# A GRU, attention, RK4 and FFN kernel: FFN pieces in new slots on all engines, a seed between two transposes, one piece ahead of the cubic term

## The reference, cut to what matters

```python
def derivative(q, p, drive, coupling, bias):
    dq = q - q ** 3 / 3.0 - p + drive + jnp.tanh(q) @ coupling.T + bias
    dp = EPSILON * (q + ALPHA - BETA * p)
# four derivatives a step (RK4), then q and p are clipped; 64 steps; q is kept
...
qx, sx, sc = reorder_quantize(q_trace, up_reorder_index)      # fp8 by row
g = qlinear(qx, sx, sc, w_gate, ...)                          # 512 -> 1408
u = qlinear(qx, sx, sc, w_up, ...)
t = jax.nn.silu(g) * u
qt, st, sct = reorder_quantize(t, down_reorder_index)
y = qlinear(qt, st, sct, w_down, down_reorder_index)          # 1408 -> 512
out = x1 + y
```

## Time and profile before

| | us |
|---|---|
| runs (3), median | 1643.82 |
| lowest, highest | 1642.74, 1644.45 |
| the profiled execution's own time | 1640.76 |
| its span | 1638.8 |

### The profile page before, as it was taken

One profiled execution on the slowest core, in us unless ns is written; L12 is line 12 of the kernel. 1 busy time (PEld: TensorE's weight loads), 2 busy tenths in 40 slices (PEclk: granted clock), 3 DMA queues, 4 the chain that ended last, 5 costly groups with the idle time before them and its releaser, 6 DMA issues.

```text
span 1638.8 us, 46339 instructions
## 1 busy us (share of the span) xinstructions
PE 1489.4 (91%) x16583; PEld 927.8 (57%) x16624; DVE 1119.8 (68%) x3565; ACT 588.7 (36%) x1903; POOL 381.5 (23%) x545
## 2 busy tenths in 40 slices
PE   5999999996799999999999997678899999999984
PEld 1333333334575767667675844556666666666662
DVE  1667667765774747575664732578888888888886
ACT  1444444441102020201102021455555555555552
POOL 0221221210000000000000000245655555556550
PEclk8999999997899999999999998999999999999996
DMA  7111112116101000100000024001111111111111
GB/s 304 44 45 50 51 46 65 51 47 167 9 1 26 0 26 0 26 0 26 6 19 13 13 64 163 21 25 29 40 40 40 33 35 32 35 32 43 37 38 33
DMA packets 91035, 72.79 MB, mean 44 GB/s; under 512 B 32480, under 2 KB 82912, under 8 KB 89824
## 3 DMA queue, kind: packets, MB, share of 16 engines
q1 hardware_dynamic: 71184, 59.35, 12.4%
q10 hardware_dynamic: 18032, 6.88, 1.7%
q0 software_dynamic: 1760, 5.77, 1.2%
HBM read 55.03 MB, written 16.94 MB: 44 GB/s over the span
## 4 chain that ended last, share of the span: by engine, by line
PE 73%; DVE 13%; ACT 5%; issue 5%; DMA 1%; POOL 1%; DVEq 0%; SPq 0%; POOLq 0%; ACTq 0%
PE ps L655 13%; PE ps L645 13%; PE ps L750 11%; PE ps L583 11%; PE ps L595 10%; PE ps L689 3%; PE ps L713 3%; ACT mem L961 3%; DVE mem L1313 2%; DVE mem L1271 2%; PE ps L740 2%; ACT ps L953 2%; PE ps L764 1%; PE ps L666 1%; DVE ps L1281 1%
## 5 line engine op out<-in xcount | busy, mean ns | idle before, releaser
L750 PE MATMUL ps<-mem 128*32 128x128 f32 x8192 | 278.8, 276 | 68.5 <-ACT mem L961 65.8
L750 PEld LDWEIGHTS ps<-mem 128*32 128x32 f32 x8192 | 211.4, 110 | 143.0 <-ACT mem L961 97.2
L645 PE MATMUL ps<-mem 128*128 128x512 f32 x512 | 224.6, 592 | 0.0
L655 PE MATMUL ps<-mem 128*128 128x256 f32 x1024 | 222.3, 379 | 0.0
L655 PEld LDWEIGHTS ps<-mem 128*128 128x128 f32 x1024 | 194.0, 190 | 26.0
L509 POOL TENSOR_TENSOR mem<-mem 128x128 f32<-128x128 f32 x64 | 30.8, 481 | 732.8 <-ACT mem L956 732.8
L583 PE MATMUL ps<-mem 128*32 128x384 f32 x2048 | 181.6, 497 | 10.2 <-DMA mem<-in_W_ih 6.3
L595 PE MATMUL ps<-mem 128*32 128x384 f32 x2048 | 177.6, 488 | 2.4 <-DVE mem L1098 2.4
L928 ACT ACTIVATE mem<-mem 128x512 f32<-128x512 f32 x32 | 19.7, 630 | 391.0 <-DVE mem L1211 391.0
L645 PEld LDWEIGHTS ps<-mem 128*128 128x128 f32 x512 | 95.6, 190 | 109.7 <-issue 109.3
L961 ACT ACTIVATE mem<-mem 128x64 f32<-128x64 f32 x512 | 102.9, 248 | 116.5 <-DVE mem L1271 116.4
(11 more groups left out here) (139 smaller groups left out, 2097.0 us busy)
## 6 DMA issues: line engine op xcount, KB each, us to landing
mem<-x_scr SPq DMA_DIRECT2D x128, 64.0 KB, 1.8
mem<-in_xT SPq DMA_DIRECT2D x64, 64.0 KB, 1.9
mem<-in_Wq SPq DMA_DIRECT2D x1, 4096.0 KB, 12.4
mem<-in_Wo SPq DMA_DIRECT2D x1, 4096.0 KB, 20.7
mem<-in_x SPq DMA_DIRECT2D x16, 256.0 KB, 2.8
x_scr<-mem SPq DMA_DIRECT2D x32, 128.0 KB, 2.3
q_scr<-mem SPq DMA_DIRECT2D x64, 64.0 KB, 1.6
mem<-q_scr SPq DMA_DIRECT2D x64, 64.0 KB, 1.9
```

Of the source, the lines that this page charges most:

```text
L645: mm = pe.matmul(ps[:, 6 + pr, :], aoT[:, h, pr * P:pr * P + P], wo[:, h, :], start=(h == 0), stop=(h == HEADS - 1))
L655: mm = pe.matmul(ps[:, h % Q_BANKS, 0:BLK], wq[:, c, h * DH:(h + 1) * DH], xnb[:, c, :], start=(c == 0), stop=(c == NC - 1))
L750: mm = pe.matmul(ps[32 * j:32 * j + 32, st % 2, 0:P], thT[:, c, :], ct[:, c, j * P:(j + 1) * P], start=False, stop=(c == NC - 1), skip_gro ...
```

## The change

The products become pieces by a table of (product, first, last matmul) for each slot. PE: slot 11 also takes two matmuls of the second product, slot 12 its other two and two of the third, slot 13 the rest; slot 0 takes one matmul of the sixth product and slot 1 three. The down product is cut 2, 5, 3, 1 instead of 3, 3, 3, 2. The parts of t change sizes (640, then 768 columns). On DVE `gate_part` 1 goes from slot 13 to 14, `t_added` 0 from 11 to 10, `t_grid` 1 from 10 to 11, `t_added` 1 from 15 to 13, `ysc` from 10 to 15. On GpSimd and ACT the matching pieces move (second `gate_scaled` and `silu_part` 14 to 15, roundings 12 to 11 and 15 to 14, the output's addition 11 to 15). SP puts the output's store and x1's loads behind the tile's loads. In the RK4, DVE does a first stage's `fill()` ahead of the cubic term, and the seed of a step's first stage between the two transposes.

```diff
-GU_SLOTS = (11, 12, 13, 15, 0, 1, 3, 4)
-DOWN_SLOTS = (5, 7, 8, 9)
-T_PARTS = ((0, 6 * P), (6 * P, INNER))
+GU_SLOTS = {11: ((0, 0, NC), (1, 0, 2)), 12: ((1, 2, NC), (2, 0, 2)), 13: ((2, 2, NC),), 15: ((3, 0, NC),),
+            0: ((4, 0, NC), (5, 0, 1)), 1: ((5, 1, NC),), 3: ((6, 0, NC),), 4: ((7, 0, NC),)}
+DOWN_SLOTS = {5: (0, 2), 7: (2, 7), 8: (7, 10), 9: (10, IC)}
+T_PARTS = ((0, 5 * P), (5 * P, INNER))
...
-                    if s == 2 and out_tile is not None:
-                        tile_store(out_tile)
-                    if s == 2 and x1_tile is not None:
-                        tile_x1(x1_tile)
                 if g is not None:
                     tile_loads(g)
+                if out_tile is not None:
+                    tile_store(out_tile)
+                if x1_tile is not None:
+                    tile_x1(x1_tile)
...
-                    if k in (13, 14):
-                        gate_scaled(i, k - 13)
+                    if k in (13, 15):
+                        gate_scaled(i, k // 15)
...
-                    if k in (12, 15) and rk:
-                        t_rounded(i, k // 15)
+                    if k in (11, 14) and rk:
+                        t_rounded(i, k // 14)
...
-                if i is not None and k == 11 and rk:
+                if i is not None and k == 15 and rk:
                     pool.wait_ge(f_ysc, i + 1)
...
-                    if k == 8:
+                    if k == 7:
                         pe.wait_ge(f_tTcp, 2 * i + 2)
                     if k in DOWN_SLOTS:
-                        down(i, DOWN_SLOTS.index(k))
+                        down(*DOWN_SLOTS[k])
...
-                    if k in (13, 14):
-                        silu_part(i, k - 13)
+                    if k in (13, 15):
+                        silu_part(i, k // 15)
...
+            def turned_half(src, half):
+
+                dve.transpose(qsT[:, 2 * half:2 * half + 2, :].rearrange("p c b -> p (c b)"), src[:, half * 64:half * 64 + 64]).then_inc(rk_qT, 1)
+
             def state_turned(src):
-
-                for half in range(2):
-                    dve.transpose(qsT[:, 2 * half:2 * half + 2, :].rearrange("p c b -> p (c b)"), src[:, half * 64:half * 64 + 64]).then_inc(rk_qT, 1)
+                turned_half(src, 0)
+                turned_half(src, 1)
...
+                if st == 0:
+                    fill()
                 dve.wait_ge(rk_sq, n + 1)
                 stt(out=ebuf, in0=ps[:, 5, 0:P], scalar=KEPT[st], in1=qs, op0=ALU.subtract, op1=ALU.mult).then_inc(rk_e, 1)
                 if st < 3:
                     seed(t, s, st + 1)
-                fill()
-                if st == 0 and not (last and s == 3):
+                if st:
+                    fill()
+                elif not end:
                     drive_sum(t + 1, (s + 1) % 4, g + 1 + (s == 3))
...
-                if not (end and st == 3):
+                if st < 3:
                     state_turned(dst)
-                if st == 3:
+                else:
                     if not end:
+                        turned_half(dst, 0)
                         seed(t + 1, (s + 1) % 4, 0)
-
+                        turned_half(dst, 1)
                     wait_if(dve, q_wr[s], PRIMED + 16 * g)
                     dve.tensor_scalar(qn[s], dst, CLAMP, -CLAMP, ALU.min, ALU.max).then_inc(rk_qs, 1)
...
-                    if k in (12, 13):
-                        if k == 12:
-                            v.need(v.n)
-                        gate_part(i, k - 12)
+                    if k == 12:
+                        v.need(v.n)
+                        gate_part(i, 0)
                     if k == 14:
+                        gate_part(i, 1)
                         gated_part(i, 0)
...
                     if k == 10:
+                        t_added(v, 0)
+                    if k == 11:
                         t_grid(v, 1)
-                    if k == 11:
-                        t_added(v, 0)
-                    if k == (15 if rk else 11):
+                    if k == (13 if rk else 11):
                         t_added(v, 1)
...
-                if i is not None and k == 10:
+                if i is not None and k == (15 if rk else 10):
                     v.need(v.n)
                     dve.wait_ge(f_y, i + 1)
```

More of the change, by code:

```diff
@@ L754, in stage, with product @@
                     mix_into(t, s, st + 1)
-            def product(i, kind, m):
-                gate, order = kind == "g", GU_ORDER.index((kind, m))
-                wait_if(pe, *{0: (f_gated, GU_T * i - 1), 1: (f_gated, GU_T * i), 2: (f_gsc, GU_T * i + 1), 3: (f_gsc, GU_T * i + 2),
-                              4: (f_gated, GU_T * i + 1), 5: (f_gsc, GU_T * i + 3), 6: (f_gated, GU_T * i + 2),
-                              7: (f_gsc, GU_T * i + 4)}[order])
-                for c in range(NC):
+            def product(i, order, lo, hi):
+                kind, m = GU_ORDER[order]
+                gate = kind == "g"
+                if lo == 0:
+                    wait_if(pe, *{0: (f_gated, GU_T * i - 1), 1: (f_gated, GU_T * i), 2: (f_gsc, GU_T * i + 1), 3: (f_gsc, GU_T * i + 2),
+                                  4: (f_gated, GU_T * i + 1), 5: (f_gsc, GU_T * i + 3), 6: (f_gated, GU_T * i + 2),
+                                  7: (f_gsc, GU_T * i + 4)}[order])
+                for c in range(lo, hi):
                     mm = pe.matmul(ps[:, 2 + order % 2, 0:GU_N], qxT[:, c, :], (wgT if gate else wuT)[:, c, m * GU_N:(m + 1) * GU_N],
                                    start=(c == 0), stop=(c == NC - 1))
-                mm.then_inc(f_g if gate else f_u, 1)
+                if hi == NC:
+                    mm.then_inc(f_g if gate else f_u, 1)
             def t_turned(i, half):
@@ L788, in slot @@
                         pe.wait_ge(f_qTcp, i + 1)
-                    if k in GU_SLOTS[:4]:
-                        product(i, *GU_ORDER[GU_SLOTS.index(k)])
+                    if k >= 11:
+                        products(i, k)
                 i = tile(1)
                 if i is not None:
-                    if k in GU_SLOTS[4:]:
-                        product(i, *GU_ORDER[GU_SLOTS.index(k)])
+                    if k < 11:
+                        products(i, k)
                     if k == 15:
@@ L803, in slot, with products, down @@
                         pe.wait_ge(f_tTcp, 2 * i + 1)
-                    if k == 8:
+                    if k == 7:
                         pe.wait_ge(f_tTcp, 2 * i + 2)
                     if k in DOWN_SLOTS:
-                        down(i, DOWN_SLOTS.index(k))
-            def down(i, part):
-                for c in range(3 * part, min(3 * part + 3, IC)):
+                        down(*DOWN_SLOTS[k])
+            def products(i, k):
+                for order, lo, hi in GU_SLOTS.get(k, ()):
+                    product(i, order, lo, hi)
+            def down(lo, hi):
+                for c in range(lo, hi):
                     mm = pe.matmul(ps[:, 7, :], t8T[:, c, :], wdT[:, c, :], start=(c == 0), stop=(c == IC - 1))
-                if part == 3:
+                if hi == IC:
                     mm.then_inc(f_y, 1)
```

## The result

| | before | after |
|---|---|---|
| median of 4 runs each, us | 1643.28 | 1624.84 |
| lowest, highest | 1640.08, 1644.45 | 1623.2, 1630.71 |
| ratio to before, 95% interval | | 0.9908, 0.9887 to 0.9928 |
| the profiled execution's own time | 1640.76 | 1630.71 |
| its span | 1638.8 | 1628.8 |

What follows compares the result with a forecast made beforehand. The prediction took a loop of dependences through PE, DVE and ACT as the bound. 13.3 us from 12 loop passes plus 3.9 outside make 17.2, off the median of 1643.82: 1626.6 us, range 1618 to 1637.

Steps and rivals of the forecast that it cites:

- The loop's term: The device loop's 12 passes: each falls from 36.27 to 35.16, 1.11 less, 13.3 us in all.
- The forecast case: Whole kernel: mask collides with GpSimd's addition but goes before its next operation, seed shortens the step's end; 1626.6 us, chance 0.52.
- The step's end: Last stage of a step: with the seed between the transposes, coupling to coupling takes 2.15 instead of 2.26.
- The second rival: At the steps' ends the seed gains nothing: 5.3 us missing, 1631.9 us, or 1636.7 with a late half; chance 0.18.
- The first stage's piece: First stages of steps: FFN piece ahead of the cubic term, so DVE is no longer late; 2.16 instead of 2.39.
- Stage 0: First stage of a pass: 2.16 plus 0.15 for a fifth product matmul, 2.31.
- The products: Second stages (1, 5, 9, 13): one or two matmuls fewer, so each takes the floor of 2.13; stage 1 had 2.25.
- Stage 8: First stage with the bit mask as its piece: mask overlaps GpSimd's addition, takes about 1.0, and the stage takes 2.72.
- The first rival: In stage 8 the mask does not collide with GpSimd's addition: stage 2.23, 5.9 us less, 1620.7 us; chance 0.15.
- The third rival: In stage 8 GpSimd's next operation goes ahead of the waiting mask: 1.43 more a pass, 1645.7 us; chance 0.07.
- GpSimd's two places: GpSimd's delayed first multiply and its longer rounding before the step's sum: 0.06 in stage 14, 0.07 in stage 15.
- Outside the loop: Four passes outside the loop: group 0 nothing, group 1 0.25, groups 2 and 15 1.8 each; together 3.9 us.

Runs made afterwards that it cites:

- seed_back: The changed kernel with its two transposes together again and the seed behind them; 1626.25 us, pass 35.36 against 35.19.
- before_piece: The kernel before with only a first stage's piece put ahead of the cubic term; 1635.27 us, beside 1641.82 for the kernel before.
- later_and_spread: Changed kernel, both masks in stage 9, grids in 10, first addition in 11, one matmul moved from stage 0 to 15, one from 7 to 6; 1616.29 us.
- mask_back: The changed kernel with stage 8's bit mask alone put back behind the cubic term and the seed; 1640.59 us, beside 1640.79 for the kernel before.

## Why the prediction was right, point by point

Forecast 1626.6 us, measured 1624.84 and, timed again, 1624.43. The loop's term was 13.3 and came out as 13.24 in one execution and 13.13 in the other. The forecast case holds: the mask does collide, GpSimd does not keep its turn, the seed does shorten the step's end.

- **The step's end**: 2.15 forecast; 2.15, 2.20, 2.16 and 2.15 measured in stages 3, 7, 11 and 15. The 0.93 from the new state to the coupling is exact. The second rival (the seed gives nothing) falls, for the step's end. But two things about the clip were off. The forecast had it "0.12 before the now earlier coupling", and it starts 0.06 before: from the first transpose to the clip, start to start, it takes 0.54 (1265.54 to 1266.08) with the seed between the transposes, and took 0.48 (1301.79 to 1302.27) with the pair in one. And the rival's price, 4 x 0.11 x 12 = 5.3 us, left out that a clip nearer to the coupling makes the next first stage longer, a loss that the seed brings and that would go with it. seed_back shows it: the four steps' ends lose 0.37 by undoing the seed, the four first stages get 0.23 back, 0.14 of it in stage 0, and with 0.02 in stage 14 about 0.17 a pass is left, 2.0 us in the loop.
- **The first stage's piece**: 2.16 forecast for stages 4 and 12, 2.15 measured, and 2.12 to 2.16 in before_piece. Right, and the later clip does not show here because the mixes start 0.34 behind the seed L1303 (as in the rows above, 1267.08 to 1267.42) and not the 0.41 that was taken as an upper bound.
- **Stage 0** was the mis-sized term: 2.31 forecast, 2.45 measured in every steady pass. Its mixes were put at +1.15 or so and start at +1.28. The working had L1303 at +0.77, and it is at +0.94 (1266.14 to 1267.08): 0.06 from the clip, and 0.12 more between clip and piece than in other stages. In stage 12 of the pass the piece starts 0.17 behind the clip, in stage 0 it starts 0.30 behind:

```profile
1257.47 0.25 DVE L1341 TENSOR_SCALAR mem<-ps 128x128 f32<-128x128 f32 x1
...
1257.64 0.56 DVE L1451 SCALAR_TENSOR_TENSOR mem<-ps,mem 128x352 f32<-128x352 f32 x1
...
1547.54 0.25 DVE L1341 TENSOR_SCALAR mem<-ps 128x128 f32<-128x128 f32 x1
...
1547.72 0.56 DVE L1451 SCALAR_TENSOR_TENSOR mem<-ps,mem 128x352 f32<-128x352 f32 x1
```

  The second pair is stage 0 of group 15, which is written out behind the loop: 0.18. The first pass, entered from above, has 0.18 too (1125.47, 1125.65), and its stage 0 takes 2.27. What sets the steady passes apart is DVE's branch back to the loop's start: the last register instruction of the loop (its line is `Fori`'s, L104) is at 1266.2 in the steady pass, behind the clip's start, and at 1125.2 in the first, ahead of it. Before, the branch lay in the 0.35 that DVE idled for ACT's square; the piece ahead of the cubic term used that cover up. A loop written out was not tried, so the branch is argued from where the 0.12 appears and where not. Against the forecast it is 0.14 x 12 = 1.7 us.
- **The products**: 2.13 forecast for stages 1, 5, 9, 13, and 2.13 in each. Stage 7: 2.18 forecast, 2.20 measured. The price of the fifth matmul in stage 0, 0.15, is shown by later_and_spread.
- **Stage 8**: 2.72 forecast, 2.67 measured, the mask 1.00 long for "about 1.0", ending 0.34 behind L539 for the 0.35 taken. The first rival (no collision) falls. The reading to the letter of the Trainium skill's rule (SBUF — State Buffer, section Who interferes with whom) was 0.1 more: the second of a pair waits until the first has ended and then runs whole, which would be 0.48 behind L539 and not 0.34. That one blocks the other for a whole instruction, and that the order of issue decides, the traces bear out: in mask_back the mask takes 1.60 for 0.48 where the subtraction goes first, and the subtraction 1.63 for 1.27 where the mask does. The 0.05 by which the stage came out shorter is the bound of 0.41 again: the mixes start at +1.60 (1283.62 to 1285.22) and not at +1.69.
- **The third rival** (GpSimd keeps its turn) falls by the rows of after, in which the waiting mask goes first in every pass. Its price was never met: 1.43 a pass was for a mask that waits from the clip on through both of GpSimd's operations. The nearest case that was run, a mask that asks just behind the subtraction (mask_back), costs 0.93.
- **GpSimd's two places**: 0.06 in stage 14 was right (2.19), and by the first of the two queues that the forecast named. In stage 13 GpSimd's L510 takes 1.02 under DVE's wide addition (in before it took 0.46 there), so its multiply L525 ends only at 1262.48; DVE's product with it, L1459, starts 0.11 behind that, and the new state L1327 at +1.28 (1261.81 to 1263.09) for +1.22:

```profile
1260.03 1.02 POOL L510 TENSOR_TENSOR mem<-mem 128x128 f32<-128x128 f32 x1 [1.60 <-ACT mem L964]
...
1261.54 0.94 POOL L525 TENSOR_TENSOR mem<-mem 128x352 f32<-128x352 f32 x1
...
1261.81 1.08 PE L751 MATMUL ps<-mem 128*32 128x128 f32 x32
...
1262.59 0.58 DVE L1459 SCALAR_TENSOR_TENSOR mem<-ps,mem 128x352 f32<-128x352 f32 x1
...
1263.09 0.28 DVE L1327 SCALAR_TENSOR_TENSOR mem<-ps,mem 128x128 f32<-128x128 f32 x1
```

  The 0.07 in stage 15, for the rounding in front of the step's sum, was nothing: 2.15 for 2.22. With stage 8's 0.05 this offsets stage 0's 0.14, so that the loop's sum comes out closer than its terms is luck.
- **Outside the loop**: 3.9 forecast. Measured 3.78 between the profiled executions, of which group 0's 0.49 is not the change's (no FFN runs in it; its second stage, partly at the lower clock, took 3.01 in one execution and 2.54 in the other, and its steps' ends 2.22 to 2.23 in both, so that the seed gives nothing there), and in the second execution of the change 4.5 (0.30, 2.08 and 2.13 for groups 1, 2 and 15, against the forecast's 0.25, 1.8 and 1.8). In the first execution, group 2 has a coupling of 1.94 us instead of 1.08, at a granted clock of 0.61. The coupling in the timeline:

```profile
1108.88 1.94 PE L751 MATMUL ps<-mem 128*32 128x128 f32 x32 [0.56 <-ACT mem L969]
```

And the window around it:

```profile
1108.00:1112.00 4.00, 3.44 (x41) 2.83 (x42) 3.08 (x13) 1.90 (x10) 1.65 (x3) 0.61 0.07 17
```

## What to carry to other kernels

When an instruction is moved earlier on an in-order engine, follow every instruction behind it to its own deadline: this seed won 0.37 in a pass at the steps' ends and gave 0.23 of it back in the first stages, since the clip behind it came nearer to the coupling. A piece moved into an engine's idle time also uses up the cover of what else was hidden there, here, as far as the rows tell, a loop's branch. And where two engines start operations that hold each other off within 0.03 us of each other, the kernel stands on an edge: any change ahead of it can cost a microsecond a pass, so put such an operation where the other engine is idle or the stage has time to spare.
